# Two chained LoRA layers in one kernel: other loading, rounding and warm-up of the first weight blocks

## The chip, the cores and the metric

The kernel runs on one core of one Trainium2 chip, with its engines TensorE (PE, matmuls), VectorE (DVE), ScalarE (ACT), GpSimdE (POOL) and SyncE (SP, which here only issues transfers), and 16 DMA engines. The metric is the device time of one execution in microseconds, 284.11 us for the kernel before (median of three runs). Lower is better.

## What is computed

Two linear layers with LoRA adapters, each added to its own input:

```
x = x + x @ W0.T + b0 + 2 * (x @ A0[i]) @ B0[i]          # i: adapter of the batch, 8 batches
x = x + x @ W1.T + b1 + (x @ A1[j].T) @ B1[j].T          # x: (8, 256, 1024) float32
```

W0 and W1 are 1024 x 1024. The kernel multiplies the two layers together first: with U = I + W0 and V = I + W1.T, the output is x times the product of the two (V taken with its identity too, U stored so that no transpose is needed) plus terms of rank 32 and biases. So the first 110 us are the product of two 1024 x 1024 matrices, and the rest multiplies x of each batch by it.

## The kernel before

**Tiling.** Both products are done by quadrants of 512 x 512 with Strassen-like sums: U has quadrants u11, u12, u21, u22, V has v11, v12, v21, v22, and the sums are called us1 to us4 and vt1 to vt4. A quadrant is held as 128 partitions x 2048 numbers, which are KH = 4 blocks k of 128 x 512. Product 1 is u11 times v11, product 2 u12 times v21, product 7 us3 times vt3, product 3 us4 times v22.

**Two parts of a number.** A matmul takes its operands rounded (fp32r). To keep float32 precision each operand is split: its high part is the rounded number, made by ScalarE (`high_first`, `high_half`, `high`; it is a plain copy to the rounded type, called CAST in the profile), and its low part is raw minus high, made by VectorE (`low_first`, `low_half`, `low`). A product is then three passes on PE: high times high (line 1065), high times low (1069), low times high (1070).

**The start, in order of time.** SP issues eight loads, u11 and v11 by turns, one 128 x 512 block each (line 302), and then six whole quadrants of 1 MB in the order u12, v21, u21, v22, v12, u22 (line 305). VectorE clears zeros (line 870, 128 x 512, then two more memsets). PE waits for the first zeros and does WARM = 8 matmuls on them, whose result nobody reads (line 1105). For each block k of u11 and v11, VectorE adds the identity to the 128 x 128 diagonal piece in place (`diagonal`, line 656), ScalarE rounds the block (line 431), VectorE makes the low part (line 661). PE waits for both high parts, does four high passes (one for each 128 columns m of u11, into banks 0 to 3), waits for both low parts and does eight low passes. The four blocks make product 1.

**What comes behind.** ScalarE rounds u12 and v21 by halves (line 435), VectorE makes their low halves (666). Then VectorE goes on in the order that its code is written in: us3 = u21 - u11 (line 674, needs u21 landed), second low half of v21, diagonal of v22, factor sums, vt3 = v12 - v22, low parts of us3 and vt3, diagonal of u22, us2, us4, bias sums, low part of us4, one addition to a bank, low part of v22 (`low("v22")`, line 671). PE's next product after product 7 is product 3, which needs the low parts of us4 and v22. Between them stand four transposes (`turn(0)`, line 1091). Nothing reorders anything: each engine does its list as written, and semaphores are the only waits. The semaphore of the rounded parts of u11 counts with `hi[SLOT["u11"]]`, that of the low parts with `lo[...]`; PARTS says how many increments a quadrant makes in its place, and `filled` adds what stood in the place before.

Of the kernel before, what the change touches and what calls it, by code (L numbers as in the profile page):

```python
# [5 lines left out]
F32 = mybir.dt.float32  # L6
# [4 lines left out]
P = 128  # L11
HALF = 512
WARM = 8
DMA = 16
# [25 lines left out]
def lora_pair(nc, xT, U11, V11, W0, W1T, A0, B0T, A1T, B1, b0, b1, idx0, idx1, out):  # L40
# [22 lines left out]
    with ExitStack() as ctx:  # L63
# [3 lines left out]
        def sem(name):  # L67
            return ctx.enter_context(nc.semaphore(name))
# [107 lines left out]
        landed = {q: sem(f"landed_{q}") for q in ("u12", "u21", "u22", "v12", "v21", "v22")}  # L176
        first_landed = {q: [sem(f"landed_{q}_{g}") for g in range(KH)] for q in ("u11", "v11")}
        lora_landed = sem("lora_landed")
        b0t_landed = sem("b0t_landed")
# [14 lines left out]
        masks_made = sem("masks_made")  # L194
        bias_zeroed = sem("bias_zeroed")
        diag_added = sem("diag_added")
# [28 lines left out]
        t_summed = sem("t_summed")  # L225
        t_zeroed = sem("t_zeroed")
        t_bounced = sem("t_bounced")
# [41 lines left out]
        def _(sp):  # L269
# [29 lines left out]

            for k in range(KH):  # L300
                for q, src in (("u11", U11), ("v11", V11)):
                    sp.dma_start(raw_k(q, k), src[k, :, :]).then_inc(first_landed[q][k], DMA)
            for q in ("u12", "v21", "u21", "v22", "v12", "u22"):
# [3 lines left out]
                             ).then_inc(landed[q], DMA)  # L307
            sp.wait_ge(bias_zeroed, 1)
            sp.dma_start(bias_sum[0:1, :], b1).then_inc(bias1_landed, DMA)
# [3 lines left out]
            sp.dma_start(t_dram, t_sum[:, :]).then_inc(t_bounced, DMA)  # L313
            sp.wait_ge(t_zeroed, 1)
            sp.wait_ge(t_bounced, DMA)
# [110 lines left out]
        @block.scalar  # L426
        def _(act):
            def high_first(k):
                for n, q in enumerate(("u11", "v11")):
                    act.wait_ge(diag_added, 2 * k + n + 1)  # L430
                    nc.scalar.copy(op_k(q, 0, k), raw_k(q, k)).then_inc(hi[SLOT[q]], 1)  # L431
# [72 lines left out]
            act.dma_start(b0_raw[:, :], b0).then_inc(b0_landed, DMA)  # L504
            for k in range(KH):
                high_first(k)
# [134 lines left out]
        def _(dve):  # L641
# [8 lines left out]
            def diagonal(k):  # L650
                for q in ("u11", "v11"):
                    dve.wait_ge(first_landed[q][k], DMA)
                    if k == 0 and q == "u11":
                        dve.wait_ge(ident_made, 2)
                    block_k = raw_k(q, k)[:, k * P:(k + 1) * P]
                    nc.vector.tensor_tensor(block_k, block_k, ident[:, :], ALU.add).then_inc(diag_added, 1)

            def low_first(k):
                for q in ("u11", "v11"):
                    dve.wait_ge(hi[SLOT[q]], filled(q, k + 1))  # L660
                    nc.vector.tensor_tensor(op_k(q, 1, k), raw_k(q, k), op_k(q, 0, k), ALU.subtract
                                            ).then_inc(lo[SLOT[q]], 1)
# [206 lines left out]

            nc.vector.memset(c_rows[:, 0:HALF].bitcast(F32), 0.0).then_inc(warm_set, 1)  # L870
            nc.vector.memset(bias_sum, 0.0).then_inc(bias_zeroed, 1)
            nc.vector.memset(t_cols[:, :], 0.0).then_inc(t_zeroed, 1)
            for k in range(KH):
                diagonal(k)
                low_first(k)
# [3 lines left out]
            dve.wait_ge(landed["u21"], DMA)  # L879
            dve.wait_ge(lo[SLOT["u11"]], filled("u11", KH))  # L880
            combine("us3", "u21", "u11", ALU.subtract)
# [175 lines left out]
        def _(pe):  # L1057
# [50 lines left out]
            for k in range(KH):  # L1108
                pe.wait_ge(hi[SLOT["u11"]], filled("u11", k + 1))
# [4 lines left out]
                pe.wait_ge(lo[SLOT["u11"]], filled("u11", k + 1))  # L1114
# [299 lines left out]
```

## Time and profile before

| | us |
|---|---|
| median of three runs (284.02 to 284.24) | 284.11 |
| the profiled execution's own time | 284.42 |
| its span, first to last instruction | 282.8 |
| PE busy in it | 278.3 (98%) |
| VectorE busy | 215.2 (76%) |
| ScalarE busy | 102.3 (36%) |

The span is what the trace shows; 1.6 us of the profiled execution's time lie around it. Times in the rows below are microseconds from the span's start.

### The profile page before, as it was taken

The numbers are of one execution on the slowest core, as the hardware profiler recorded it, in microseconds if no ns is written. First come the engines' busy times: TensorE is split into PE (matmuls) and PEld (weight loads), VectorE is DVE, ScalarE is ACT, GpSimd is POOL, SyncE is SP. The second block draws the span as 40 slices with busy tenths as digits, with TensorE's granted clock in tenths as the row PEclk, the third lists the DMA queues.
The fourth block names the chain that finished last, engine by engine and source line by source line (L and its number), as shares of the span: only waits on it lengthen the run. The fifth ranks groups of instructions, "written<-read, shape, count | busy, mean of one in ns | idle before, by whom it ended". The sixth has DMA issues, their size and how long they took to land.

```text
span 282.8 us, 3853 instructions
## 1 busy us (share of the span) xinstructions
PE 278.3 (98%) x1319; PEld 224.5 (79%) x1319; DVE 215.2 (76%) x318; ACT 102.3 (36%) x141; POOL 19.3 (7%) x45
## 2 busy tenths in 40 slices
PE   7999999999999999999999999999999999999995
PEld 5888888888868887877888878888878888878885
DVE  5789999999899899967975873865873875865413
ACT  4565464262965574322331231141221131321100
POOL 3333200400000001000000100000000000000000
PEclk9999999999999999999999999999999999999999
DMA  6997000100365400451622802712701712212002
GB/s 217 391 409 309 31 1 2 57 19 0 129 230 211 139 14 19 158 185 76 206 74 76 261 37 75 236 46 80 249 37 74 239 43 93 75 39 86 25 37 111
DMA packets 13095, 33.92 MB, mean 120 GB/s; under 512 B 2149, under 2 KB 2405, under 8 KB 13078
## 3 DMA queue, kind: packets, MB, share of 16 engines
q1 hardware_dynamic: 11906, 31.60, 31.6%
q0 software_dynamic: 1024, 2.10, 2.3%
q8 instruction: 10, 0.16, 0.2%
q14 instruction: 7, 0.06, 0.1%
q10 hardware_dynamic: 148, 0.00, 0.0%
HBM read 22.09 MB, written 11.60 MB: 119 GB/s over the span
## 4 chain that ended last, share of the span: by engine, by line
PE 98%; DVE 0%; issue 0%
PE bank L1227 18%; PE bank L1228 18%; PE bank L1229 18%; PE bank L1065 9%; PE bank L1069 9%; PE bank L1070 9%; PE bank L1258 3%; PE bank L1234 3%; PE bank L1083 1%; PE bank L1105 1%; PE bank L1097 1%; PE bank L1099 1%; PE bank L1098 1%; PE bank L1085 1%; PE bank L1084 1%; PE bank L1167 1%
## 5 line engine op out<-in xcount | busy, mean ns | idle before, releaser
L1227 PE MATMUL bank<-ops,late 128*128 128x512 f32 x192 | 75.5, 393 | 0.0
L1228 PE MATMUL bank<-ops,late 128*128 128x512 f32 x192 | 74.9, 390 | 0.0
L1229 PE MATMUL bank<-ops,late 128*128 128x512 f32 x192 | 74.8, 389 | 0.0
L1069 PE MATMUL bank<-ops 128*128 128x512 f32 x112 | 43.8, 391 | 0.0
L1070 PE MATMUL bank<-ops 128*128 128x512 f32 x112 | 43.6, 390 | 0.0
L1227 PEld LDWEIGHTS bank<-ops,late 128*128 128x128 f32 x192 | 36.1, 188 | 9.5 <-issue 2.1
L1229 PEld LDWEIGHTS bank<-ops,late 128*128 128x128 f32 x192 | 36.1, 188 | 7.7
L1228 PEld LDWEIGHTS bank<-ops,late 128*128 128x128 f32 x192 | 36.1, 188 | 7.4
L1065 PE MATMUL bank<-ops 128*128 128x512 f32 x112 | 41.1, 401 | 0.0
L484 ACT CAST late<-rows 128x512 fp32r<-128x512 f32 x24 | 14.7, 622 | 52.3 <-DVE rows L762 26.0
L484 ACT CAST late<-raw_a 128x512 fp32r<-128x512 f32 x24 | 14.8, 624 | 30.6 <-PE bank L1234 21.1
L1065 PEld LDWEIGHTS bank<-ops 128*128 128x128 f32 x112 | 21.4, 192 | 5.1 <-ACT ops L431 0.7
L1070 PEld LDWEIGHTS bank<-ops 128*128 128x128 f32 x112 | 21.2, 189 | 4.5
L1069 PEld LDWEIGHTS bank<-ops 128*128 128x128 f32 x112 | 21.2, 189 | 4.5
L671 DVE TENSOR_TENSOR ops<-raw_a,ops 128x2048 fp32r<-128x2048 f32 x9 | 20.6, 2284 | 0.6 <-ACT ops L438 0.6
L745 DVE TENSOR_TENSOR late<-rows,late 128x512 fp32r<-128x512 f32 x24 | 16.6, 691 | 5.0 <-ACT late L484 4.8
L438 ACT CAST ops<-raw_a 128x2048 fp32r<-128x2048 f32 x9 | 17.2, 1916 | 6.7 <-DVE raw_a L674 3.6
L745 DVE TENSOR_TENSOR late<-raw_a,late 128x512 fp32r<-128x512 f32 x24 | 16.3, 687 | 3.8 <-ACT late L484 3.7
L849 DVE TENSOR_TENSOR raw_a<-bank,raw_a 128x512 f32<-128x512 f32 x8 | 5.5, 692 | 17.8 <-PE bank L1234 17.8
L438 ACT CAST ops<-raw_b 128x2048 fp32r<-128x2048 f32 x6 | 11.4, 1916 | 6.8 <-DVE raw_b L674 3.5
L671 DVE TENSOR_TENSOR ops<-raw_b,ops 128x2048 fp32r<-128x2048 f32 x6 | 13.6, 2284 | 0.0
L405 POOL DMA_DIRECT2D a_raw<-A x8 | 4.3, 542 | 130.1 <-DVE aa L790 128.1
(153 smaller groups left out, 379.4 us busy)
## 6 DMA issues: line engine op xcount, KB each, us to landing
raw_a<-xT SPq DMA_DIRECT2D x16, 512.0 KB, 4.8
out<-raw_a SPq DMA_DIRECT2D x27, 256.0 KB, 2.0
a<-rb_rows SPq DMA_DIRECT2D x8, 392.0 KB
raw_a<-W1T SPq DMA_DIRECT2D x2, 1024.0 KB, 12.6
raw_b<-W SPq DMA_DIRECT2D x2, 1024.0 KB, 16.3
rb_rows<-b_hl SPq DMA_DIRECT2D x3, 512.0 KB
rb_rows<-late SPq DMA_DIRECT2D x3, 512.0 KB
raw_a<-U SPq DMA_DIRECT2D x4, 256.0 KB, 4.4
```

Source lines behind the costliest of these rows:

```text
L438: nc.scalar.copy(op(q, 0), raw(q)).then_inc(hi[SLOT[q]], 1)
L484: nc.scalar.copy(x_op(j, 0), x_raw(j, b)).then_inc(op_hi[j], 1)
L671: nc.vector.tensor_tensor(op(q, 1), raw(q), op(q, 0), ALU.subtract).then_inc(lo[SLOT[q]], 1)
L745: nc.vector.tensor_tensor(x_op(j, 1), x_raw(j, b), x_op(j, 0), ALU.subtract).then_inc(op_lo[j], 1)
L1065: return mm(bank[:, :], left(u, 0, k, m), op_k(v, 0, k), start=(k == 0 and not on_top), stop=False, skip_group_check=on_top)
L1069: mm(bank[:, :], left(u, 0, k, m), op_k(v, 1, k), start=False, stop=False, skip_group_check=on_top)
L1070: return mm(bank[:, :], left(u, 1, k, m), op_k(v, 0, k), start=False, stop=(k == KH - 1), skip_group_check=on_top)
L1227: mm(bank[:, :], hi, t_op(t, 0, k), start=(start and k == 0), stop=False, skip_group_check=not start)
L1228: mm(bank[:, :], hi, t_op(t, 1, k), start=False, stop=False, skip_group_check=not start)
L1229: last = mm(bank[:, :], lo, t_op(t, 0, k), start=False, stop=(k == KH - 1), skip_group_check=not start)
L1234: return mm(bank[:, :], h_stack[b % 2][0:STACK, q * P:(q + 1) * P], rb[b % 2][:, h * HALF:(h + 1) * HALF], start=False, stop=True, skip_gr ...
L1258: last = mm(banks[6 + s][j * CT:(j + 1) * CT, 0:T], aa[:, s, k, :], xr[s][:, 2 * kh:2 * kh + 2, tok], start=(k < TILES), stop=(k >= KT - T ...
```

## The change

The first blocks (k = 0) of u11 and v11 are handled by code of their own; blocks 1 to 3 go as before, with counts moved by one.

- SP loads v11's block 0 first, then u11's block 0 as two halves of 128 x 256 with a semaphore each, then blocks 1 to 3 as before. The first part has nine transfers in place of eight.
- VectorE clears 128 columns of zeros first and the other 384 in a second memset. `bias_zeroed` and `t_zeroed` become one semaphore.
- PE does four short matmuls of 128 columns on the first zeros, and then WARM = 6 of 512 columns, in place of eight.
- VectorE adds the identity to the diagonal piece and writes the sum rounded straight into the high part (two pieces of 128 x 128), ScalarE rounds the other columns (384 of v11; 128 and 256 of u11) and no longer waits for VectorE. After that VectorE also adds the identity in place, which the low parts read.
- PE's waits for block 0 are for half of u11 each.

```diff
-WARM = 8
+WARM = 6
+WARM_SHORT = 4
-PARTS = {"u11": KH, "v11": KH, "u12": 2, "v21": 2, "d21": KH, "d22": KH}
+PARTS = {"u11": KH + 1, "v11": KH, "u12": 2, "v21": 2, "d21": KH, "d22": KH}
@@ SP
-            for k in range(KH):
+            sp.dma_start(raw_k("v11", 0), V11[0, :, :]).then_inc(first_landed["v11"][0], DMA)
+            for n, done in ((0, first_landed["u11"][0]), (1, u11_half_landed)):
+                cols = slice(n * HALF // 2, (n + 1) * HALF // 2)
+                sp.dma_start(raw_k("u11", 0)[:, cols], U11[0, :, cols]).then_inc(done, DMA)
+            for k in range(1, KH):
@@ ScalarE
+            def first_block():
+                act.wait_ge(first_landed["v11"][0], DMA)
+                nc.scalar.copy(op_k("v11", 0, 0)[:, P:HALF], raw_k("v11", 0)[:, P:HALF]).then_inc(hi[SLOT["v11"]], 1)
+                for landed_n, cols in ((first_landed["u11"][0], slice(P, HALF // 2)),
+                                       (u11_half_landed, slice(HALF // 2, HALF))):
+                    act.wait_ge(landed_n, DMA)
+                    nc.scalar.copy(op_k("u11", 0, 0)[:, cols], raw_k("u11", 0)[:, cols]).then_inc(hi[SLOT["u11"]], 1)
@@ VectorE
+            def first_block():
+                dve.wait_ge(ident_made, 2)
+                for q in ("v11", "u11"):
+                    dve.wait_ge(first_landed[q][0], DMA)
+                    nc.vector.tensor_tensor(op_k(q, 0, 0)[:, 0:P], raw_k(q, 0)[:, 0:P], ident[:, :], ALU.add
+                                            ).then_inc(diag_added, 1)
+                for n, (q, cols) in enumerate((("v11", slice(0, HALF)), ("u11", slice(0, HALF // 2)))):
+                    block = raw_k(q, 0)[:, 0:P]
+                    nc.vector.tensor_tensor(block, block, ident[:, :], ALU.add).then_inc(diag_added, 1)
+                    dve.wait_ge(diag_added, n + 3)
+                    dve.wait_ge(hi[SLOT[q]], 1)
+                    nc.vector.tensor_tensor(op_k(q, 1, 0)[:, cols], raw_k(q, 0)[:, cols], op_k(q, 0, 0)[:, cols],
+                                            ALU.subtract).then_inc(lo[SLOT[q]], 1)
...
-            nc.vector.memset(c_rows[:, 0:HALF].bitcast(F32), 0.0).then_inc(warm_set, 1)
+            for cols in (slice(0, P), slice(P, HALF)):
+                nc.vector.memset(c_rows[:, cols].bitcast(F32), 0.0).then_inc(warm_set, 1)
@@ PE
+            for _ in range(WARM_SHORT):
+                mm(banks[7][:, 0:P], c_rows[:, 0:P], c_rows[:, 0:P], start=True, stop=True)
+            pe.wait_ge(warm_set, 2)
...
+            pe.wait_ge(diag_added, 2)
+            pe.wait_ge(hi[SLOT["v11"]], 1)
+            for m in range(KH):
+                if m % 2 == 0:
+                    pe.wait_ge(hi[SLOT["u11"]], m // 2 + 1)
+                high_pass("u11", "v11", a_banks[m], m, 0)
+            pe.wait_ge(lo[SLOT["v11"]], 1)
+            for m in range(KH):
+                if m % 2 == 0:
+                    pe.wait_ge(lo[SLOT["u11"]], m // 2 + 1)
+                low_passes("u11", "v11", a_banks[m], m, 0)
```

The order of the transfers that SP issues at the very start, before the change; raw_a holds u quadrants, raw_b v11, and 128x2x1024 is a whole quadrant:

```order
L302 DMA raw_a<-U11 128x512
L302 DMA raw_b<-V11 128x512
L302 DMA raw_a<-U11 128x512
L302 DMA raw_b<-V11 128x512
L302 DMA raw_a<-U11 128x512
```

and in the changed kernel:

```order
L303 DMA raw_b<-V11 128x512
L306 DMA raw_a<-U11 128x256 x2
L309 DMA raw_a<-U11 128x512
L309 DMA raw_b<-V11 128x512
L309 DMA raw_a<-U11 128x512
```

V11's block has changed places with U11's, which is two transfers now, so each later load is issued as number n + 1.

VectorE's list from its first instruction to the diagonal of block 1, before:

```order
L870 MEMSET c_rows 128x512
L871 MEMSET rows 128x1024
L872 MEMSET t_cols 32x8
L656 TENSOR_TENSOR raw_a<-raw_a,ident 128x128 [waits ident_made,landed_u11_0]
L656 TENSOR_TENSOR raw_b<-raw_b,ident 128x128 [waits landed_v11_0]
L661 TENSOR_TENSOR ops<-raw_a,ops 128x512 [waits hi_of_place0]
L661 TENSOR_TENSOR ops<-raw_b,ops 128x512 [waits hi_of_place1]
L656 TENSOR_TENSOR raw_a<-raw_a,ident 128x128 [waits landed_u11_1]
```

and in the changed kernel (hi_of_place0 counts the rounded parts of u11, hi_of_place1 those of v11):

```order
L908 MEMSET c_rows 128x128
L908 MEMSET c_rows 128x384
L909 MEMSET rows 128x1024
L910 MEMSET t_cols 32x8
L678 TENSOR_TENSOR ops<-raw_b,ident 128x128 [waits landed_v11_0,ident_made]
L678 TENSOR_TENSOR ops<-raw_a,ident 128x128 [waits landed_u11_0]
L682 TENSOR_TENSOR raw_b<-raw_b,ident 128x128
L685 TENSOR_TENSOR ops<-raw_b,ops 128x512 [waits hi_of_place1,diag_added]
L682 TENSOR_TENSOR raw_a<-raw_a,ident 128x128
L685 TENSOR_TENSOR ops<-raw_a,ops 128x256 [waits hi_of_place0,diag_added]
L689 TENSOR_TENSOR ops<-raw_a,ops 128x256 [waits hi_of_place0]
L671 TENSOR_TENSOR raw_a<-raw_a,ident 128x128 [waits landed_u11_1]
```

Two instructions on 128 x 128 are added for block 0, and one low part is cut in two. Behind that VectorE's list is the same in both; here it is at the place where it comes to us3 = u21 - u11, in the changed kernel:

```order
L703 TENSOR_TENSOR ops<-raw_a,ops 128x1024 [waits hi_of_place2] x2
L703 TENSOR_TENSOR ops<-raw_a,ops 128x1024 [waits hi_of_place3]
L711 TENSOR_TENSOR raw_a<-raw_b,raw_a 128x2048 [waits lo_of_place0,landed_u21]
L703 TENSOR_TENSOR ops<-raw_a,ops 128x1024 [waits hi_of_place3]
L663 TENSOR_TENSOR raw_a<-raw_a,ident 128x128 [waits landed_v22]
```

Nothing moved there: us3 still stands between the two low halves of v21 (hi_of_place3) and waits for the landing of u21.

## Rows read from the trace of the kernel before

**Rows 1.** The page: busy us, share of the span, instructions of the engine.

```profile
PE 278.3 (98%) x1319; PEld 224.5 (79%) x1319; DVE 215.2 (76%) x318; ACT 102.3 (36%) x141; POOL 19.3 (7%) x45
```

**Rows 2.** The timeline's start: start us, us, engine, line, operation [idle before <-releaser].

```profile
0.99 0.39 SPq L302 DMA_DIRECT2D raw_a<-U  x1
1.16 0.48 DVE L870 MEMSET c_rows<- 128x512 f32 x1 [1.16 <-PEq L1404]
...
1.43 0.42 SPq L302 DMA_DIRECT2D raw_b<-V  x1
...
1.70 3.78 PE L1105 MATMUL bank<-c_rows 128*128 128x512 f32 x8 [1.70 <-DVE c_rows L870]
...
3.81 0.29 DVE L656 TENSOR_TENSOR raw_a<-raw_a,ident 128x128 f32<-128x128 f32 x1 [1.08 <-DMA raw_a<-U]
4.13 0.62 ACT L431 CAST ops<-raw_a 128x512 fp32r<-128x512 f32 x1 [0.64 <-DVE raw_a L656]
...
4.42 0.29 DVE L656 TENSOR_TENSOR raw_b<-raw_b,ident 128x128 f32<-128x128 f32 x1 [0.32 <-DMA raw_b<-V]
...
4.74 0.62 ACT L431 CAST ops<-raw_b 128x512 fp32r<-128x512 f32 x1
4.79 0.69 DVE L661 TENSOR_TENSOR ops<-raw_a,ops 128x512 fp32r<-128x512 f32 x1
...
5.47 1.35 PEld L1065 LDWEIGHTS bank<-ops 128*128 128x128 f32 x4 [0.72 <-ACT ops L431]
...
7.05 0.62 ACT L431 CAST ops<-raw_b 128x512 fp32r<-128x512 f32 x1
...
7.35 0.59 PE L1069 MATMUL bank<-ops 128*128 128x512 f32 x1
...
7.78 0.40 PE L1070 MATMUL bank<-ops 128*128 128x512 f32 x1
...
8.01 0.40 PE L1069 MATMUL bank<-ops 128*128 128x512 f32 x1
```

**Rows 3.** Groups by line and form, 0 to 20 us: xcount | busy us, mean ns.

```profile
L435 ACT CAST ops<-raw_a 128x1024 fp32r<-128x1024 f32 x4 | 4.1, 1059 | 0.9 <-DMA raw_a<-W 0.9
```

**Rows 4.** Start of v21's first half and of product 2: ACT, PE and PEld.

```profile
16.22 1.05 ACT L435 CAST ops<-raw_a 128x1024 fp32r<-128x1024 f32 x1
...
17.36 1.32 PEld L1065 LDWEIGHTS bank<-ops 128*128 128x128 f32 x6
```

**Rows 5.** Line 305's load v21 (issued at 5.43 us), then load u21 (5.95).

```profile
DMA to landing us min/median/max: 10.3/10.3/10.3
...
DMA to landing us min/median/max: 12.6/12.6/12.6
```

**Rows 6.** Timeline of VectorE from 17 us, around us3 = u21 - u11 (line 674).

```profile
17.31 1.23 DVE L666 TENSOR_TENSOR ops<-raw_a,ops 128x1024 fp32r<-128x1024 f32 x1 [1.03 <-ACT ops L435]
18.58 2.29 DVE L674 TENSOR_TENSOR raw_a<-raw_b,raw_a 128x2048 f32<-128x2048 f32 x1
20.79 1.22 DVE L666 TENSOR_TENSOR ops<-raw_a,ops 128x1024 fp32r<-128x1024 f32 x1
```

**Rows 7.** Timeline from 42 us: low part of v22 (VectorE), transposes and product 3 (PEld).

```profile
42.52 2.28 DVE L671 TENSOR_TENSOR ops<-raw_a,ops 128x2048 fp32r<-128x2048 f32 x1
...
44.61 0.58 PEld L1091 LDWEIGHTS bank<-ident,g_all 128*128 128x128 f32 x4
45.16 0.19 PEld L1065 LDWEIGHTS bank<-ops 128*128 128x128 f32 x1
```

**Rows 8.** Stretches: length, PE, PEld, DVE, ACT, POOL busy (count), PEclk, DMA share, GB/s.

```profile
4.80:5.20 0.40, 0.40 (x2) 0.00 (x0) 0.40 (x1) 0.40 (x1) 0.00 (x0) 1.00 0.59 138
...
12.00:18.50 6.50, 6.50 (x31) 5.37 (x30) 4.32 (x5) 4.77 (x7) 2.32 (x5) 1.00 1.03 415
...
18.60:45.20 26.60, 26.60 (x122) 21.96 (x120) 26.24 (x26) 13.34 (x15) 4.82 (x9) 1.00 0.34 130
```

More of the change, by code:

```diff
@@ L504, in _ @@
             act.dma_start(b0_raw[:, :], b0).then_inc(b0_landed, DMA)
-            for k in range(KH):
+            first_block()
+            for k in range(1, KH):
                 high_first(k)
@@ L652, in diagonal, with first_count @@
                     dve.wait_ge(first_landed[q][k], DMA)
[L653 to L654 removed]
                     block_k = raw_k(q, k)[:, k * P:(k + 1) * P]
                     nc.vector.tensor_tensor(block_k, block_k, ident[:, :], ALU.add).then_inc(diag_added, 1)
+            def first_block():
[11 more added lines that the diff above has]
+                                            ALU.subtract).then_inc(lo[SLOT[q]], 1)
+                cols = slice(HALF // 2, HALF)
+                dve.wait_ge(hi[SLOT["u11"]], 2)
+                nc.vector.tensor_tensor(op_k("u11", 1, 0)[:, cols], raw_k("u11", 0)[:, cols], op_k("u11", 0, 0)[:, cols],
+                                        ALU.subtract).then_inc(lo[SLOT["u11"]], 1)
+            def first_count(q, k):
+                return filled(q, k + PARTS[q] - KH + 1)
             def low_first(k):
                 for q in ("u11", "v11"):
[L660 removed]
+                    dve.wait_ge(hi[SLOT[q]], first_count(q, k))
                     nc.vector.tensor_tensor(op_k(q, 1, k), raw_k(q, k), op_k(q, 0, k), ALU.subtract
@@ L868, in put_c12 @@
                 nc.vector.tensor_tensor(c12[b % 2], W[:, :], u4[b % 2], ALU.add).then_inc(made["c12"], 1)
-            nc.vector.memset(c_rows[:, 0:HALF].bitcast(F32), 0.0).then_inc(warm_set, 1)
-            nc.vector.memset(bias_sum, 0.0).then_inc(bias_zeroed, 1)
-            nc.vector.memset(t_cols[:, :], 0.0).then_inc(t_zeroed, 1)
-            for k in range(KH):
+            for cols in (slice(0, P), slice(P, HALF)):
+                nc.vector.memset(c_rows[:, cols].bitcast(F32), 0.0).then_inc(warm_set, 1)
+            nc.vector.memset(bias_sum, 0.0).then_inc(zeroed, 1)
+            nc.vector.memset(t_cols[:, :], 0.0).then_inc(zeroed, 1)
+            first_block()
+            for k in range(1, KH):
                 diagonal(k)
@@ L879, in _ @@
             dve.wait_ge(landed["u21"], DMA)
-            dve.wait_ge(lo[SLOT["u11"]], filled("u11", KH))
+            dve.wait_ge(lo[SLOT["u11"]], first_count("u11", KH - 1))
             combine("us3", "u21", "u11", ALU.subtract)
@@ L1103, in _ @@
             pe.wait_ge(warm_set, 1)
+            for _ in range(WARM_SHORT):
+                mm(banks[7][:, 0:P], c_rows[:, 0:P], c_rows[:, 0:P], start=True, stop=True)
+            pe.wait_ge(warm_set, 2)
             for _ in range(WARM):
                 mm(banks[7][:, :], c_rows[:, 0:P], c_rows[:, 0:HALF], start=True, stop=True)
-            for k in range(KH):
-                pe.wait_ge(hi[SLOT["u11"]], filled("u11", k + 1))
+            pe.wait_ge(diag_added, 2)
[9 more added lines that the diff above has]
+                low_passes("u11", "v11", a_banks[m], m, 0)
+            for k in range(1, KH):
+                pe.wait_ge(hi[SLOT["u11"]], filled("u11", k + 2))
                 pe.wait_ge(hi[SLOT["v11"]], filled("v11", k + 1))
@@ L1113, in _ @@
                         high_pass("u11", "v11", a_banks[m], m, k)
-                pe.wait_ge(lo[SLOT["u11"]], filled("u11", k + 1))
+                pe.wait_ge(lo[SLOT["u11"]], filled("u11", k + 2))
                 pe.wait_ge(lo[SLOT["v11"]], filled("v11", k + 1))
```

10 lines of the change are left out of this document (5 added, 5 removed).

## The prediction

> **What bounds the kernel now.** I read the page's busy times first: PE is busy for 278.3 us of a span of 282.8 [rows 1], so whatever shortens or delays PE's list is seen in the time, and nothing else is. Then the timeline of the first 8 us, since every edit lies there: look at what each engine waits for. PE's first work is eight matmuls on zeros from 1.70 us, its first useful weight load is at 5.47, and what released it is ScalarE's rounding of v11's block 0, which ended at 4.74 + 0.62 = 5.36 [rows 2]. That is the wait which the change attacks. Last I followed the engines behind it to 45 us, to ask who would hold PE if it came earlier. Two places have little room, at product 2 [rows 4, 5] and at product 3 [rows 6, 7], and the second one decides the forecast.
>
> **First part: zeros and warm-up.** The memset of 512 columns takes 0.48 us and PE starts 0.06 behind it [rows 2]. For 128 columns the bounds are a quarter, 0.12, and the 0.29 of VectorE's 128-column addition; I take 0.17, so PE starts near 1.4 in place of 1.70. Matmuls of 512 columns lie 0.43 us apart here, as 7.35 to 7.78 shows [rows 2]; six of them are 2.6 us. Four short ones have no row; they cost between a quarter of 0.43 each and the whole of it, 0.4 to 1.7 us, and since they move a quarter of the columns I take 0.6. Warm-up then ends near 1.4 + 0.6 + 2.6 = 4.6. It is hidden as long as the useful work isn't ready before that (4.74, next part); at the dear end it would end at 5.7, 0.25 behind today's 5.47, and the time would be near 284.3.
>
> **Second part: the first useful matmul.** V11's block takes the place of U11's and lands when that did, 0.99 + 2.8 = 3.8 us, where VectorE started on it [rows 2]. Half of u11 is issued at 1.43; the whole v11 block issued then landed at 4.42, so the half lands between 3.8 and 4.42, I take 4.1. VectorE's two diagonal pieces are 0.29 each: 3.81 to 4.10, and on to 4.40. ScalarE's cast takes 0.62 for 512 columns and 1.06 for 1024 [rows 2, 3], that is 0.18 + 0.86 ns a column: 0.51 for 384, 0.29 for 128. It runs 3.83 to 4.34 and 4.34 to 4.63. PE followed ScalarE by 0.11 before (5.36 to 5.47), so its first useful weight load comes at 4.74: **0.73 us earlier**. With the half landing at 4.42 it would be 5.0.
>
> Not all of that is kept. The granted clock column reads 1.00 from the start [rows 8], but the matmuls' spacing tells two levels: 0.43 us up to 7.78, which is the 1.2 GHz level for 512 columns, and 0.23 behind it, the 2.4 GHz level. PE had been busy without a long pause since 1.70. If the rise stays near 7.6, the matmuls come at about 4.8, 5.3, 5.8, 6.2, 6.6, 7.1, 7.5, and the eighth at 7.8; before, the eighth was at 8.01 + 0.23 = 8.24 (the sixth stands at 7.78). So 0.45 of the 0.73 is left. If the rise moves with PE's first matmul, 0.3 earlier, it is 0.55. I take **0.5 us**.
>
> The Trainium skill, "TensorE: Matmul & The Clock Gate", Part 1, says that the window by which the clock is released runs freely and does not restart with the kernel, so that the moment of the rise varies from run to run. No row here shows a spread of that moment; the three runs lie within 0.22 us of each other. By that rule the 0.5 could be anything from a loss to more than 1 us. It is the last rival below.
>
> **Third part: what covers the added work.** For block 0 VectorE gets two additions more (2 x 0.29) and a low part in two pieces. Its low part of v11 runs about 4.7 to 5.4 (0.69, the row of 4.79 [rows 2]), the in-place diagonal of u11 to 5.7, the first low half of u11 to 6.1, the second to 6.5. It used to be at block 1's diagonal by 5.40 + 0.69 = 6.09, so it is up to 0.4 late there. PE comes to the low passes at 6.6 and needs the first low half then: 0.5 of cover. Block 1 was rounded by 7.05 + 0.62 = 7.67 [rows 2], up to 0.4 later now, 8.1; PE comes to it eight matmuls after the fifth, near 7.78 + 7 x 0.23 - 0.5 = 8.9. Covered, at no cost. The merged semaphore costs nothing: SP waits for it with nothing queued that anyone needs soon.
>
> **Fourth part: product 2.** v21 lands at 5.43 + 10.3 = 15.7 [rows 5]. ScalarE rounded its first half from 16.22 to 17.27, behind a copy that waits for PE, and PE's weight load for product 2 was at 17.36 [rows 4]. With PE earlier, ScalarE can begin at 15.73, no sooner: 15.73 + 1.05 + 0.11 = 16.9 in place of 17.36. PE's gain is at most **0.47 us** from here on.
>
> **Fifth part: product 3, the bound.** VectorE's low half of v21 is 17.31 + 1.23 = 18.54; instructions behind each other overlap by 0.08 to 0.1 (18.58 + 2.29 is 20.87, the next starts at 20.79), so us3 could have started at 18.44. It started at 18.58 [rows 6]. It waits for u21, and u21 landed at 5.95 + 12.6 = 18.55 [rows 5]. A transfer's landing doesn't move when PE does. From there VectorE works without a stop, 26.24 of 26.60 us busy [rows 8], up to the low part of v22, which ends at 42.52 + 2.28 = 44.80; PE's first weight load of product 3, which needs it, is at 45.16, after four transposes that would come earlier [rows 7]. With a handover of 0.06 to 0.11 (the memset's and ScalarE's above) it can come at 44.88 at the soonest. So of PE's 0.5 only 45.16 - 44.88 = **0.28 us** survives. PE then stands waiting for the rest, about 0.2 us.
>
> **Sixth part: is u21 later?** SP issues nine transfers in place of eight, so u21's issue moves back by one slot, 1.43 - 0.99 = 0.44 us, and its landing by d. High end: the whole slot, 0.44. Low end: DMA engines are full from before the first landing, share 1.03 at 12 to 18.5 us, so issue is not what they wait for: 0. Below zero: at 4.8 to 5.2 us the share is 0.59 [rows 8], an idle 0.16 that another order might fill: -0.16. I take d = 0.1, near the row of full engines and a little for the transfer's halves. The Trainium skill, "DMA: Bandwidth & Descriptors", its table at the top, puts the smallest row for full rate at 512 bytes, and the halves have rows of 1 KB; by that d would be 0 and the sum 283.83. No run here shows it yet.
>
> **The sum.** 0.28 - 0.1 = 0.18 us less. The profiled execution (284.42, span 282.8) would give 284.24, span 282.6. It lies 0.3 above the median of the runs, so against that: 284.11 - 0.18 = **283.93 us**. A measurement of this kernel can tell about 0.2%, 0.57 us, from no change, so this is no change.
>
> **The rivals.** (a) *VectorE isn't tied to u21*: us3 starts sooner with PE's earlier v21, and PE keeps product 2's 0.47 less d, 0.37: 283.74. For it: us3 waited only 0.14 us. Against: the landing and the start agree to 0.03. Still within 0.2%. (b) *The whole front moves*: the clock is up by the first useful matmul and both landings come sooner too. Block 1 to 3's chain on VectorE and ScalarE would then bound, some 1.4 us before today's: 282.7. Nothing makes a landing sooner; needed are two things at once. (c) *Slower, by u21's landing*: at line 674 each microsecond that u21 lands later passes through VectorE to product 3 and into the time. The gain is gone at d = 0.28; with the whole slot, 0.44, it is 284.27; over 0.2% slower it is from d = 0.85, two slots. For it: the transfer engines are full, so lost time is never made up. Against: they lose only what the halves cost. (d) *The clock rises later*: each further matmul at the low level costs 0.2 us; PE's spare is 0.5 - 0.18 = 0.3, so it decides from the second matmul on; with eight more, PE is 1.6 - 0.5 = 1.1 us late: 285.2.
>
> **How the numbers follow.** Forecast 0.78, (a) 0.10, (b) 0.03, (c) beyond 0.2% 0.06, (d) 0.03. Predicted is the likeliest, 283.9. The range takes in the ends of d (283.67 with -0.16, 284.27 with the slot), the dear short matmuls (284.3) and (a): 283.6 to 284.4. Faster by over 0.2%: (b) and a little, 0.04. Slower: (c) and (d), 0.09. Within: 0.87.
>
> **What would show it.** In the changed kernel's timeline: first useful weight load near 4.7; its matmuls at 0.43 spacing up to about 7.6; product 2's first weight load near 16.9; us3 at VectorE's line 711 at 18.6 to 18.7 and not before; a wait of PE of some 0.2 us for line 708's low part of v22 ahead of product 3, near 44.9. I am wrong if us3 starts before 18.5, or u21's landing has moved by over 0.5, or if the spacing falls to 0.23 at another time by more than 2 us.

## The result and the profile after

The changed kernel's median is 285.18 us in 22 executions (284.21 to 288.27), against 284.29 us in 22 of the kernel before beside it (283.77 to 285.77). The ratio is 1.0028, 95% interval 1.0015 to 1.0041. So it is slower by 0.28%, with an interval that is clear of 1; predicted was 283.9 with a range to 284.4. The profiled execution took 285.24 us, 0.8 more than the one before. Its span is only 0.1 longer than before's, so this pair of traces alone can't carry the explanation: span and time of one execution vary by about as much as the effect. Where the text below compares sizes it uses the median span of a kernel's executions: 283.10 us after, 282.50 to 282.65 before in the four batches of experiments.

The page of the changed kernel, busy times (answering to [rows 1]):

```profile
span 282.9 us, 3865 instructions
...
PE 277.7 (98%) x1321; PEld 223.6 (79%) x1321; DVE 215.9 (76%) x322; ACT 102.2 (36%) x142; POOL 19.2 (7%) x45
```

Its start on the timeline of PE, PEld, ScalarE and SP's queue (start us, us, engine, line, operation, idle before and what ended it). This answers to [rows 2]:

```profile
1.30 1.12 PE L1144 MATMUL bank<-c_rows 128*128 128x128 f32 x4 [1.30 <-DVE c_rows L908]
...
4.46 0.54 PEld L1104 LDWEIGHTS bank<-ops 128*128 128x128 f32 x2
...
4.81 0.63 PE L1104 MATMUL bank<-ops 128*128 128x512 f32 x2
6.03 0.74 PE L1104 MATMUL bank<-ops 128*128 128x512 f32 x2 [0.59 <-ACT ops L442]
6.61 0.40 PE L1108 MATMUL bank<-ops 128*128 128x512 f32 x1
6.84 0.39 PE L1109 MATMUL bank<-ops 128*128 128x512 f32 x1
...
1.43 0.89 SPq L306 DMA_DIRECT2D raw_a<-U  x2
...
3.61 0.51 ACT L438 CAST ops<-raw_b 128x384 fp32r<-128x384 f32 x1
4.03 0.29 ACT L442 CAST ops<-raw_a 128x128 fp32r<-128x128 f32 x1
5.57 0.40 ACT L442 CAST ops<-raw_a 128x256 fp32r<-128x256 f32 x1 [1.25 <-DMA raw_a<-U]
```

The first useful weight load is at 4.46 in place of 5.47: the edit does what it is for. Then comes what no part of the prediction had. The second half of u11's block, issued near 1.90, landed at about 5.55; ScalarE had waited 1.25 us for it, and PE, having done two of the four high passes, stood until 6.03.

Product 2 and line 711 (answering to [rows 4, 6]): ScalarE, PEld and VectorE.

```profile
16.40 1.05 ACT L451 CAST ops<-raw_a 128x1024 fp32r<-128x1024 f32 x1 [0.75 <-DMA raw_a<-W1T]
17.35 1.56 ACT L530 COPY raw_b<-bank 128x512 f32<-128x512 f32 x3
...
17.51 0.30 PEld L1104 LDWEIGHTS bank<-ops 128*128 128x128 f32 x2 [0.88 <-issue]
17.98 0.30 PEld L1104 LDWEIGHTS bank<-ops 128*128 128x128 f32 x2 [0.17 <-ACT raw_b L530]
...
18.89 2.29 DVE L711 TENSOR_TENSOR raw_a<-raw_b,raw_a 128x2048 f32<-128x2048 f32 x1 [0.18 <-DMA raw_b<-W]
```

The landings behind them are those of line 312's loads v21, issued at 6.00, and u21, issued at 6.52 (answering to [rows 5]):

```profile
DMA to landing us min/median/max: 10.4/10.4/10.4
...
DMA to landing us min/median/max: 12.3/12.3/12.3
```

v21 lands at 16.4 in place of 15.7, u21 at 18.8 in place of 18.55. PE was through with product 1 at 16.45 + 0.23 = 16.68, 0.68 before the 17.36 of [rows 4], and waited 0.88 us. It even started later, at 17.51. Behind v21's cast stand three copies of banks on ScalarE (line 530) that don't need v21 at all; they came late with it, and PE waited for them three times more, by 0.17, 0.19 and 0.19.

VectorE's low part of v22 runs until 42.84 + 2.28 = 45.12 (44.80 in [rows 7]); in this execution the transposes are late enough themselves that product 3 doesn't wait:

```profile
42.84 2.28 DVE L708 TENSOR_TENSOR ops<-raw_a,ops 128x2048 fp32r<-128x2048 f32 x1
...
44.71 0.58 PEld L1130 LDWEIGHTS bank<-ident,g_all 128*128 128x128 f32 x4
45.26 0.19 PEld L1104 LDWEIGHTS bank<-ops 128*128 128x128 f32 x1
```

From there on nothing differs. In all 18 traces of this case but one the span is 237.6 to 237.7 us longer than the start of product 3's first weight load (before: 282.8 - 45.16; after: 282.9 - 45.26). The exception is named below. So every question on the time is the question when product 3 starts.

### The profile page after: what moved, and what is told of

It is laid out like the page before. It is cut to its first block, busy times and chain, and to the rows that moved or that the text cites. A ratio compares the mean times of both kernels' runs of the same rounds, so it can differ in the third digit from the quotient of the medians.

```text
span 282.9 us, 3865 instructions
## 1 busy us (share of the span) xinstructions
PE 277.7 (98%) x1321; PEld 223.6 (79%) x1321; DVE 215.9 (76%) x322; ACT 102.2 (36%) x142; POOL 19.2 (7%) x45
## 4 chain that ended last, share of the span: by engine, by line
PE 97%; DMA 1%; SPq 0%; issue 0%; DVE 0%; ACT 0%
PE bank L1280 18%; PE bank L1281 18%; PE bank L1282 18%; PE bank L1104 9%; PE bank L1109 9%; PE bank L1108 9%; PE bank L1311 3%; PE bank L1287 3%; PE bank L1122 1%; PE bank L1136 1%; PE bank L1138 1%; PE bank L1137 1%; DMA raw_a<-U 1%; PE bank L1124 1%; PE bank L1123 1%; PE bank L1220 1%
## 5 line engine op out<-in xcount | busy, mean ns | idle before, releaser
L1104 PEld LDWEIGHTS bank<-ops 128*128 128x128 f32 x112 | 20.7, 189 | 6.8 <-issue 1.3
L1109 PEld LDWEIGHTS bank<-ops 128*128 128x128 f32 x112 | 21.0, 188 | 4.5
L1108 PEld LDWEIGHTS bank<-ops 128*128 128x128 f32 x112 | 21.0, 188 | 4.4
## 6 DMA issues: line engine op xcount, KB each, us to landing
raw_b<-W SPq DMA_DIRECT2D x2, 1024.0 KB, 16.4
```

Of the source, the lines that this page charges most:

```text
L1104: return mm(bank[:, :], left(u, 0, k, m), op_k(v, 0, k), start=(k == 0 and not on_top), stop=False, skip_group_check=on_top)
L1108: mm(bank[:, :], left(u, 0, k, m), op_k(v, 1, k), start=False, stop=False, skip_group_check=on_top)
L1109: return mm(bank[:, :], left(u, 1, k, m), op_k(v, 0, k), start=False, stop=(k == KH - 1), skip_group_check=on_top)
```

## The experiments

All variants compute the whole result. Each was timed in turns with the kernel before on the same chip. "Span" is the median over its 11 or 12 executions (five for the late b0 of the changed kernel). The letters in the expectations stand for theories of the cause: A, the split of u11's block 0 does the harm; B, it lies around the span; C, the small load of b0 on ScalarE's queue collides with the new order; D and F, short rows are slow wherever they are; E, a ninth transfer costs; G, it is the split's place at the very start; H, the harm passes through u21's landing; I, K, PE's hole and the clock.

| kernel | ratio (95%) | span us |
|---|---|---|
| before, again | 1.0001 (0.9987 to 1.0015) | 282.60 |
| after, again | 1.0027 (1.0010 to 1.0044) | 283.50 |
| after, u11's block 0 whole | 0.9995 (0.9977 to 1.0012) | 282.35 |
| the same again | 0.9992 (0.9979 to 1.0006) | 282.45 |
| before, column halves at block 0 | 1.0019 (0.9998 to 1.0040) | 283.00 |
| before, row halves at block 0 | 1.0063 (1.0038 to 1.0087) | 284.50 |
| before, column halves at block 3 | 0.9999 (0.9983 to 1.0015) | 282.55 |
| before, short rows, eight transfers | 1.0015 (0.9996 to 1.0033) | 282.75 |
| before, b0 late / b0 twice | 1.0006 / 1.0003 (both across 1) | 282.70 / 282.60 |
| after, b0 late | 1.0040 (1.0025 to 1.0055) | 283.20 |
| after, whole and b0 late | 0.9999 (0.9986 to 1.0013) | 282.50 |
| before, new warm-up alone | 0.9998 (0.9984 to 1.0011) | 282.50 |
| after, old warm-up | 1.0025 (1.0010 to 1.0040) | 283.40 |
| after, whole, four bias sums moved | 1.0028 (1.0006 to 1.0051) | 283.25 |
| before, 256 KB more ahead of u21 | 1.0009 (0.9990 to 1.0028) | 282.90 |

### Both kernels again

No edit.

> The kernel before, unchanged, timed against itself. Every theory expects a ratio of 1.000; how far its interval reaches tells what a ratio of 1.001 or 1.002 in the other runs is worth.

> The changed kernel once more. The ratio measured is 1.0028, 0.8 us, but its profiled execution has a span of 282.9 against 282.8. Theory A (the halves): the nine transfers make v21 land late, product 2 starts late, and other executions are worse than the profiled one; then the spans of its runs lie 0.3 to 0.8 above those of before. Theory B (around the span): the spans are nearly equal and the time between them and the device time is longer by 0.5 us or more.

284.49 and 285.14 us: the result repeats. The time around the span is 1.75 us in the median for the one and 1.71 for the other (1.73 in the kernel before beside them), so the difference lies inside the span, and theory B falls. The two traces show at product 3 what the fifth part described (before again, then the changed kernel again: PEld; then VectorE's line 711 in the latter):

```profile
44.20 0.58 PEld L1091 LDWEIGHTS bank<-ident,g_all 128*128 128x128 f32 x4
44.94 0.19 PEld L1065 LDWEIGHTS bank<-ops 128*128 128x128 f32 x1 [0.16 <-issue]
```

```profile
44.96 0.58 PEld L1130 LDWEIGHTS bank<-ident,g_all 128*128 128x128 f32 x4
45.68 0.19 PEld L1104 LDWEIGHTS bank<-ops 128*128 128x128 f32 x1
```

```profile
19.38 2.29 DVE L711 TENSOR_TENSOR raw_a<-raw_b,raw_a 128x2048 f32<-128x2048 f32 x1 [0.43 <-DMA raw_b<-W]
```

Where PE doesn't wait, product 3 follows the start of the transposes by 0.55 to 0.56 ([rows 7]: 44.61 to 45.16). Here it follows by 0.74 and 0.72, and 0.07 behind the end of v22's low part (44.87 and 45.61). Over all traces product 3 starts, within 0.03, at the later of transposes + 0.55 and low part + 0.07, and from us3's start to the end of that low part it is 26.22 to 26.24 (but in the one variant that changes VectorE's list). So u21's landing sets a floor: product 3 comes no sooner than 26.30 after us3's start.

### The second half taken back

```diff
-            for n, done in ((0, first_landed["u11"][0]), (1, u11_half_landed)):
-                cols = slice(n * HALF // 2, (n + 1) * HALF // 2)
-                sp.dma_start(raw_k("u11", 0)[:, cols], U11[0, :, cols]).then_inc(done, DMA)
+            sp.dma_start(raw_k("u11", 0), U11[0, :, :]).then_inc(first_landed["u11"][0], DMA)
```

The other wait of ScalarE names the same semaphore; everything else of the change stays.

> The changed kernel with u11's block 0 loaded in one transfer, so eight transfers as before. Theory A: v21 lands near 15.7 and u21 near 18.55 again, the useful matmuls of block 0 have no hole, product 3 begins 0.28 us earlier than before, and the time is 0.998 to 1.000 of before, 0.8 us less than the changed kernel. Theory B: the landings go back, the time stays at 1.002 or more.

> The changed kernel with u11's block 0 whole, once more, to join with the first measurement (0.9995, span 282.35). With u21's landing where it was, PE's earlier start is cut off at product 3: 0.998 to 1.000.

0.9995 and 0.9992; spans 0.15 to 0.3 under before's and 0.65 to 1.15 under the changed kernel's in its two comparisons. PE's first useful weight load is at 4.81 in the first trace, and nothing waits in block 0 as at 6.03. The ratio's interval no longer meets that of the changed kernel with its old warm-up beside it (1.0010 to 1.0040 against 0.9979 to 1.0006). So the changed kernel's loss is all in the split of one 256 KB transfer, and without it the change gives about what the sum foretold with d near 0 (0.28 us less), too little to be told from nothing.

### The split alone, put into the kernel before

```diff
+                    if k == 0 and q == "u11":
+                        for n in range(2):
+                            cols = slice(n * HALF // 2, (n + 1) * HALF // 2)
+                            sp.dma_start(raw_k(q, k)[:, cols], src[k, :, cols]).then_inc(first_landed[q][k], DMA)
+                        continue
...
-                    dve.wait_ge(first_landed[q][k], DMA)
+                    dve.wait_ge(first_landed[q][k], 2 * DMA if k == 0 and q == "u11" else DMA)
```

> The kernel before with nothing changed but u11's block 0 loaded as two halves, both awaited before its diagonal. Theory A: the first useful matmul is late by 0.5 to 1.2 us, v21 lands at about 16.4, u21 at 18.9, and the time is 1.002 to 1.004 of before, as slow as the changed kernel or slower. Theory B: under 1.001, unless the ninth transfer itself is what lengthens the time around the span.

Span 283.00, 0.35 above before's, ratio 1.0019 with an interval that just reaches 1. But the 12 spans are two groups: seven at 282.3 to 283.2, five at 284.2 to 284.8. The profiled one is of the second. PE's timeline there:

```profile
3.15 2.33 PE L1110 MATMUL bank<-c_rows 128*128 128x512 f32 x5
6.21 2.05 PE L1070 MATMUL bank<-ops 128*128 128x512 f32 x4 [0.72 <-ACT ops L436]
8.05 0.63 PE L1074 MATMUL bank<-ops 128*128 128x512 f32 x1
8.48 0.63 PE L1075 MATMUL bank<-ops 128*128 128x512 f32 x1
...
10.61 0.46 PE L1074 MATMUL bank<-ops 128*128 128x512 f32 x1
10.91 0.40 PE L1075 MATMUL bank<-ops 128*128 128x512 f32 x1
```

The matmuls lie 0.43 apart, the 1.2 GHz level, up to 10.61 and not to 7.78 as in [rows 2]. v11's block is rounded 0.7 later here (5.45 on ScalarE in place of 4.74), so PE stands some 0.7 us between warm-up and first useful work, and in 5 of 12 executions about 2 us are lost (group medians 284.6 and 282.7); the one of them that has a trace shows a late rise of the clock. This is rival (d)'s mechanism, in a kernel that isn't the changed one. It is not what slows the changed kernel: v21 landed at 15.90 here and u21 at 18.81, theory A had 16.4 and 18.9, and us3 started only at 20.17, because PE was late. The seven executions without the loss are at before's level (282.65). So in this order of loads the split alone showed no loss through u21's landing that can be told.

### Split by rows

```diff
+                            rows_n = slice(n * P // 2, (n + 1) * P // 2)
+                            sp.dma_start(raw_k(q, k)[rows_n, :], src[k, rows_n, :]).then_inc(first_landed[q][k], DMA)
```

Two transfers of 64 partitions with rows of 2 KB, in the place of the column halves.

> The kernel before with u11's block 0 as two transfers of 64 partitions each, rows of 2 KB as ever: a ninth transfer without short rows. Theory E (one transfer more costs a slot): a slot of 0.44 us, span 283.0 as with the column halves (283.00 there, 282.65 before), ratio 1.001 to 1.002. Theory F (the short rows cost): rows are as before, so 282.65 and ratio 1.000.

The worst of all: 1.0063, and 10 of 12 spans at 284.2 to 285.2. The trace has the same late rise (0.43 spacing up to 10.74). So the length of a row isn't what makes a split at the start dear. SP's queue also took longer over these two transfers: v11's block was issued at 2.26, after column halves at 1.90, in the kernel before at 1.43. Yet u21 landed at 18.91, no later than in most traces of the changed kernel.

### The same split at block 3, and short rows without a ninth transfer

The first is the split of above with `k == 3` for `k == 0`. The second loads u11's blocks 2 and 3 as a left and a right half of both:

```diff
+                    if k >= 2 and q == "u11":
+                        cols = slice((k - 2) * HALF // 2, (k - 1) * HALF // 2)
+                        sp.dma_start(raw_k(q, 2, 2).rearrange("p (g n) -> p g n", n=HALF)[:, :, cols],
+                                     src[2:4, :, cols].rearrange("g p n -> p g n")).then_inc(first_landed[q][k], DMA)
```

> The kernel before with the column halves at u11's block 3 and not at block 0. Theory G (it is the place: at the start nothing is queued that hides a slow transfer, and PE's clock waits on it too): by 3.8 us the transfer engines have a backlog, so 282.65 and ratio 1.000. Theory E or F: the same loss as at block 0, 0.3 us or more.

> The kernel before with u11's blocks 2 and 3 loaded as their left halves in one transfer and their right halves in the next: still eight transfers, but 512 rows of 1 KB, twice as many as in the changed kernel. No matmul of block 0 is touched. Theory E: no slot more, 282.65, ratio 1.000. Theory F: the transfers take longer, u21 lands 0.3 to 1 us later, span 283.0 to 283.6, ratio 1.001 to 1.004.

Block 3's split costs nothing (0.9999, span 282.55 against 282.50). Its ninth transfer moved u21's issue to 6.20 as well, yet u21 landed at 18.30 and us3 started at 18.35: here neither the slot on SP's queue nor the halves delayed the landing. Short rows at blocks 2 and 3 gave 1.0015 with an interval across 1 and a span 0.25 longer; that one is inconclusive. What stands out is the place. The stretch 2.00 to 4.40 us of four kernels: before, after, halves at block 3, row halves at block 0 (columns as in [rows 8]: length, busy by engine, granted clock, DMA share, GB/s):

```profile
2.00:4.40 2.40, 2.40 (x6) 1.85 (x6) 1.01 (x3) 1.55 (x2) 0.68 (x2) 1.00 0.82 283
```

```profile
2.00:4.40 2.40, 2.40 (x7) 1.98 (x8) 1.44 (x5) 1.99 (x3) 0.68 (x2) 1.00 0.74 219
```

```profile
2.00:4.40 2.40, 2.40 (x6) 1.87 (x6) 1.15 (x4) 1.74 (x2) 0.68 (x2) 1.00 0.88 296
```

```profile
2.00:4.40 2.40, 2.40 (x6) 1.85 (x6) 0.74 (x3) 1.28 (x1) 0.68 (x2) 1.00 0.72 175
```

The five traces with column halves at block 0 have 212 to 230 GB/s here, row halves 175, and of the twelve with that block whole eleven have 272 to 300; one, with the bias sums moved, has 243, which nothing explains. The 65 GB/s or so that are missing for 2.4 us are 0.16 MB, which takes an estimated 0.4 us at the 400 GB/s that the changed kernel's stretch of 8 to 12 us shows. The rate in this stretch doesn't fix the landing, though: row halves had the lowest rate of all, and u21 landed at 18.91 there, against 19.17 to 19.71 in three of the four traces of the changed front. The hole is sharp: at 4.00 to 4.40 us the changed kernel moved 20 GB/s at a share of 0.34, the kernel before 311 at 1.00.

The Trainium skill, "DMA: Bandwidth & Descriptors", its table at the top, has full rate from 512 bytes. Block 3's halves, issued at 3.79 and about 4.26, had landed by about 8.2, and at 4.40 to 8.40 us that kernel moved 364 GB/s, where the kernel before and the one with the new warm-up moved 335 and 369: the trace agrees. With twice as many short rows at blocks 2 and 3 that stretch had 288, so it isn't always so. At block 0 two halves with rows of 1 KB cost a quarter of the rate (219 against 283), and two with rows of 2 KB over a third (175): what the rule says of rows isn't refuted, but it doesn't say that a split costs nothing, and here it did cost.

### The load of b0

b0 is a load of a few KB that ScalarE's queue issues at the start, among the first blocks. It was moved behind (in both kernels and in the variant with u11 whole), or issued twice.

```diff
-            act.dma_start(b0_raw[:, :], b0).then_inc(b0_landed, DMA)
...
+            act.dma_start(b0_raw[:, :], b0).then_inc(b0_landed, DMA)
```

> The changed kernel with one thing moved: ScalarE issues the small load of the bias b0 (128 rows of 32 bytes) behind its casts of the first blocks, not before them. Theory C (rows, not bytes, feed the transfer engines): at the start each transfer of 128 rows takes about 0.47 us to be handed out whatever its bytes; the two halves and b0's load are three of them for 0.26 MB, so the engines run dry (39 to 113 GB/s at 3.8 to 4.6 us). With b0 moved, u11's second half lands near 4.9 in place of 5.57, u21 0.3 to 0.5 us earlier, and the span falls by 0.3 to 0.5 from 283.1: ratio 1.000 to 1.002 of before. Theory D (the 1 KB rows themselves are slow, b0 has no part in it): landings and span as in the changed kernel, ratio 1.0028.

> The kernel before with b0's load moved in the same way. Theory C: the dip at 4.8 to 5.2 us goes, u21 lands 0.2 to 0.4 us sooner, span 282.3 to 282.5 in place of 282.65. Theory D: no difference.

> Changed kernel, u11's block 0 whole, and b0's load moved. Theory C: the best of the set, span 281.9 to 282.2, ratio 0.997 to 0.999. Theory D: as with the whole block alone, 282.35.

> The kernel before with b0 loaded a second time, to a place nobody reads, right behind the first: the suspected cost doubled. Theory C: another 128 rows are another 0.3 to 0.5 us, u21 lands near 19.0 and the span is 283.0 to 283.2, ratio 1.001 to 1.002. Theory D: 4 KB more are nothing, ratio 1.000.

1.0040, 1.0006, 0.9999 and 1.0003: it neither cures the changed kernel nor harms the others. Some 0.3 us of the 1.0040 lie around the span (2.07 in the median of five executions, against 1.72 beside them); the span is 0.6 above before's 282.60. ScalarE on the second half of u11's block in that kernel:

```profile
5.07 0.40 ACT L442 CAST ops<-raw_a 128x256 fp32r<-128x256 f32 x1 [0.68 <-DMA raw_a<-U]
```

It starts at 5.07 in place of 5.57, as theory C had it, and PE's weight loads wait 0.31 us for it in place of 1.03. But u21 landed at 19.17 and the time was no better. So theory C falls for the time, and with it the rival that the hole in PE's block 0 is what makes the changed kernel slow: most of the hole is gone here and the loss isn't. One trace is a warning: the one of before with b0 late has u21's landing at 19.8, over a microsecond later than the other traces of that front, in a kernel whose median is that of before. The landing of u21 varies from execution to execution.

### u21 later, with nothing touched ahead of it

```diff
+                if q == "u21":
+                    sp.dma_start(aa_room[:, HALF:2 * HALF], U11[0, :, :]).then_inc(idle_landed, DMA)
```

The kernel before, with 256 KB that nobody reads loaded between v21 and u21.

> The kernel before with 256 KB more loaded between v21 and u21, to a place nobody reads; everything ahead of it is untouched. Theory H (u21's landing sets product 3 and with it the time): 0.64 us more at 410 GB/s, us3 starts near 19.2, low v22 ends near 45.45, product 3's weight load is 0.06 to 0.11 behind that, and the span rises by 0.45 to 0.65 to 283.0 to 283.2; ratio 1.0015 to 1.0025. Theory I (the landing has slack and the changed kernel's loss is PE's hole in block 0): span 282.5 to 282.7, ratio 1.000.

Span 282.90, 0.3 over before's in the same batch; the ratio, 1.0009, can't be told from 1. That lies between what theory H had (283.0 to 283.2) and theory I (282.5 to 282.7), so the time decides nothing. u21 landed at 18.78, 0.2 later than in the two traces of before (18.55 and 18.58) and not the 0.64 expected. How a landing is passed on is plain in its trace, since the clock rose early in it and PE was ahead. VectorE's us3, its low part of v22, then PEld:

```profile
18.84 2.29 DVE L677 TENSOR_TENSOR raw_a<-raw_b,raw_a 128x2048 f32<-128x2048 f32 x1 [1.41 <-DMA raw_b<-W]
...
42.80 2.28 DVE L674 TENSOR_TENSOR ops<-raw_a,ops 128x2048 fp32r<-128x2048 f32 x1
...
43.47 0.58 PEld L1095 LDWEIGHTS bank<-ident,g_all 128*128 128x128 f32 x4
45.15 0.19 PEld L1069 LDWEIGHTS bank<-ops 128*128 128x128 f32 x1 [1.10 <-issue]
```

PE was 1.14 us earlier at the transposes than in [rows 7] (44.61) and lost all of it at product 3, 0.07 behind 45.08. In this execution an earlier PE was worth nothing; u21's landing decided.

### That wait taken away

In the variant with u11 whole, four bias sums of VectorE that stand between us3 and the low part of v22 were moved behind it:

```diff
-            bias_first(0)
-            bias_first(1)
...
+            bias_first(0)
+            bias_first(1)
```

> The changed kernel with u11's block 0 whole, and VectorE's first four bias sums (2.65 us, ahead of the low parts that product 3 waits for) moved behind the fourth addition and the copy of g. If VectorE's chain from u21's landing is what holds product 3, low v22 ends near 42.5, product 3's weight load stands 0.55 us behind the transposes' first (44.2 to 44.6), and the span is 0.1 to 0.4 below 282.35: 282.0 to 282.2, ratio 0.998 to 0.999. If not, nothing changes.

The low part ends 0.56 sooner (44.44, us3 18.76) and product 3 no longer waits (transposes 44.15, weight load 44.71). But the ratio is 1.0028 and the span 0.8 to 0.9 longer than with the sums in place. Here alone the span is 239.0 longer than product 3's start: VectorE, late with its sums, is waited for further on, as two groups of PEld show that have no such wait on VectorE with the sums in place:

```profile
L1308 PEld LDWEIGHTS bank<-raw_a,aa 128*32 128x32 f32 x128 | 3.6, 109 | 4.8 <-DVE aa L824 1.5 <-issue 1.4
L1119 PEld LDWEIGHTS bank<-ops,a 128*128 128x128 f32 x16 | 3.0, 187 | 1.6 <-DVE ops L705 1.0
```

A miss: the work wasn't spare there, only its place was.

### The warm-up alone, and the change without it

```diff
-WARM = 8
+WARM = 6
+WARM_SHORT = 4
...
-            nc.vector.memset(c_rows[:, 0:HALF].bitcast(F32), 0.0).then_inc(warm_set, 1)
+            for cols in (slice(0, P), slice(P, HALF)):
+                nc.vector.memset(c_rows[:, cols].bitcast(F32), 0.0).then_inc(warm_set, 1)
```

The second kernel is the changed one with these lines taken back.

> The kernel before with the new zeros and warm-up alone (128 columns cleared first, four short and six long matmuls). It ends near 4.9 us, so PE stands still for some 0.6 us before its first useful matmul at 5.4 to 5.5, not 0.2. Theory J (the clock's rise is put off by a hole in PE's work): part of the executions rise late, a cluster of spans 1.5 to 2 us longer, as with a late block 0, and the mean ratio is 1.001 to 1.003. Theory K (the hole is too short to matter): 1.000.

> The changed kernel with the old zeros and the eight long matmuls. They end at 5.3, 0.4 behind the first block (4.7), so the first useful matmul is late by that; the landings are as in the changed kernel. Theory H: u21's landing decides, so the time is that of the changed kernel, 1.002 to 1.003. Theory I: 0.2 to 0.4 us slower than it, 1.003 to 1.005.

0.9998 and 1.0025: the new warm-up has no part in it, though in the first kernel PE stands still between it and the first useful matmul, 0.40 us by its rows:

```profile
5.48 1.47 PE L1067 MATMUL bank<-ops 128*128 128x512 f32 x4 [0.40 <-ACT ops L432]
```

None of the 12 spans (282.0 to 283.1) is of the late group. A pause of 0.40 did not bring the late rise; in the traces with pauses of 0.72 and 0.85, by the same rows, it came.

## Why the prediction was wrong

**What bounds the kernel: right**, and sharper than I had it: the span is product 3's start plus 237.7.

**First and second part (zeros, first useful matmul): right in direction and size.** PE starts at 1.30 (I had 1.4), the six long warm-up matmuls begin at 2.22, the first useful weight load is at 4.46 (I had 4.74). But I costed the block by its first half only. I had put the first half's landing between 3.8 and 4.42, took 4.1, and it came near 3.9; the second half's I never asked for, and the steps "5.3, 5.8, 6.2" for PE's matmuls took it as there. It landed at 5.55. Of 1.0 us at the start, the hole of 0.59 (1.03 on the weight loads) took its share; the clock then rose by 6.4 in this execution, sooner than the 7.6 that I had put in, and gave it back. PE was ready 0.68 early at product 2, against the 0.5 forecast; that these two misses cancelled is luck.

**Third part (cover of the added work): right for VectorE, not for block 1.** VectorE was ready for block 1's diagonal at 6.44 and waited 0.47 us for the transfer, so its extra additions cost nothing. But block 1 of u11 landed at 6.87 (6.10 before), v11's block was rounded by 8.49 where I had 8.1, and PE's matmuls of block 1, for which it was ready near 8.43, began at 8.63. The cover was gone because of the transfers, another 0.2 us that no term had.

**Fourth part (product 2): mechanism right, size wrong.** PE's gain does end at v21's landing. But that was 16.4 and not 15.7, so PE's weight load came at 17.51, not 16.9. I also missed the three copies behind v21's cast on ScalarE, which cost PE another 0.55 us in sum: 0.17 + 0.19 + 0.19.

**Fifth part (product 3): right.** Nine of the 18 traces show PE waiting there for the end of the low part of v22, and us3 follows u21's landing within 0.1 us, except in the two variants of before where PE was late.

**Sixth part (d): the step that failed.** I took d = 0.1, with 0.44 as its high end, "near the row of full engines and a little for the transfer's halves". us3's start, which follows the landing, is at 18.89, 19.38, 19.21 and 19.77 in the four traces of kernels with the changed front, 19.3 in the mean. In the eleven with that block whole and no further load of size (b0's outlier of 19.81 among them) it is 17.8 to 19.8, 18.6 in the mean. So d is about 0.7. The sum 0.28 - d gives 0.4 later in place of 0.18 sooner; the spans say 0.5 (283.10 against 282.50 to 282.65 in other batches) to 0.85 (283.50 against 282.65 in one). The argument was that the engines are full, share 1.03 [rows 8], and so don't wait. It took that row from 12 us on, and the one idle stretch that I looked at, 4.80 to 5.20, I read as room for a gain. The transfers that the change cuts run at 2 to 4.4 us, where the kernel before had 283 GB/s against 385 at 8 to 12 us: the engines are not at their full rate yet, so the order and the cut of what they get can matter. That time lost there is never made up, because they are full afterwards, I wrote down myself, under rival (c). It fits the changed front, but isn't shown as a rule: with u11's halves ahead of v11, in the two variants of before, u21 landed at 18.81 and 18.91, some 0.2 to 0.3 over the mean of the kernels with the block whole, at early rates as low or lower.

So the traces bear out **rival (c)**, by u21's landing. I had it over 0.2% slower only from d = 0.85; with d near 0.7 it is already 0.28% slower, by the ratio. What makes up the difference isn't settled: by these means of few traces d is known to some 0.3 only, and where PE is the later one at product 3, as in the trace of after, the late copies of product 2 and the hole in block 0 count as well. **Rival (a)** falls: in all fifteen of those traces us3 started within 0.1 us of the landing. **Rival (d)** did not happen in the traces of the changed kernel (none has the 0.43 spacing beyond 7.9 us; one span of 22, 286.7, has no trace and is unexplained), but it did in the two variants of before.

**The range** was too narrow for a second reason. Its ends came from d's bounds around one execution, while one kernel's executions alone span 2 us (283.8 to 285.8 before).

What stays open: why a split of the first transfers lowers the rate. One transfer is issued every 0.47 us, and with 128 KB in a slot in place of 256 the queue hands over 280 GB/s, less than the engines can move. That was only argued. Row halves are of 128 KB too and fared worse than column halves; a part of that is on record, since SP's queue spent 1.27 us on the two (0.99 to 2.26) and 0.91 on column halves. Open as well is why the split delayed u21 by some 0.7 us behind v11's block and by no more than 0.3 ahead of it. No variant beat the kernel before by more than its measurement can tell; the nearest is the change without the split (0.9992 and 0.9995).

## What to carry to other kernels

Before cutting the first transfer to let an engine start on half of it, ask what the transfer engines do in the microseconds around it: if they are not yet fed and are full afterwards, time lost there can come out at a later load that something waits for, as it did in the changed kernel. Cost the second half's landing with the first's. And follow not only the engine that becomes earlier but what stands queued behind each wait that it meets, here copies behind a cast.

## What the runs showed of the hardware

- The rate at which the first transfers run depends on how they are cut: at 2.00 to 4.40 us 272 to 300 GB/s in eleven of twelve traces with 256 KB each (243 in one), 212 to 230 with one in column halves, 175 in row halves. The column cut at the seventh transfer cost nothing (364 GB/s at 4.40 to 8.40 us, against 335 and 369 without it).
- The moment at which the matmuls' spacing falls from 0.43 to 0.23 us, to the 2.4 GHz level, varies between executions: before 6 us in two variants of the kernel before (extra load, halves at block 3: the first four useful matmuls, from 5.47 and from 5.36, took 1.0 us), 7.8 in [rows 2]. The Trainium skill, "TensorE: Matmul & The Clock Gate", Part 1, says that it varies, since the window runs freely; the traces agree. In the two early ones PE waited at product 3 for VectorE, so the early rise gave nothing.
- With a pause of 0.72 and of 0.85 us ahead of the first useful matmul the rise came near 10.7 us in both traces, and 5 and 10 of 12 executions were some 1.5 to 2 us longer; with 0.40 none of 12 was. That these executions had the late rise too is inferred from their spans. The granted clock column read 1.00 in these stretches too; the spacing of the matmuls is what tells the level.
- One load's landing varied by 2 us between single executions of kernels with nearly the same front (17.8 to 19.8 for u21), far more than most edits of this size.
